# A graph-attention kernel in which the ORs of a mask check stand between a run's other steps, and chunk 0 masks a unit before it compares the next

## The reference: what is computed

```python
# layer 0: 4 heads of 32 features
Wh = (h @ W).reshape(N, H, D)
e = s_src[:, None, :] + s_dst[None, :, :]
e = where(e >= 0, e, 0.2 * e)
e = where(adj[:, :, None] > 0, e, -9e15)
attention = softmax(e, axis=1)
x = layernorm(x + elu(einsum('ijh,jhd->ihd', attention, Wh)))
# layer 1: one head of 128 features, between logmap0 and expmap0
e = leaky_relu(wh1 + wh2.T, 0.2)
attention = softmax(where(adj > 0, e, -9e15), axis=1)
x = layernorm(x + proj(expmap0(attention @ x_tan)))
```

## Time and profile before

| | |
|---|---|
| runs | 971.72, 972.5, 977.3 us; median 972.5 |
| profiled execution, its own time | 975.74 us |
| its span | 974.0 us |
| PE busy in the span | 856.1 us (88%) |
| DVE busy | 769.9 us (79%) |
| ACT busy | 674.0 us (69%) |
| mean granted TensorE clock | 0.956 |

### The profile page before, as it was taken

One profiled execution on the slowest core, in us unless ns is written; L12 is line 12 of the kernel. 1 busy time (PEld: TensorE's weight loads), 2 busy tenths in 40 slices (PEclk: granted clock), 3 DMA queues, 4 the chain that ended last, 5 costly groups with the idle time before them and its releaser, 6 DMA issues.

```text
span 974.0 us, 24352 instructions
## 1 busy us (share of the span) xinstructions
PE 856.1 (88%) x10868; PEld 698.2 (72%) x10868; DVE 769.9 (79%) x1312; ACT 674.0 (69%) x789; POOL 43.3 (4%) x80
## 2 busy tenths in 40 slices
PE   8468999989999899999998994899999999879890
PEld 6467999989999899999997952455555555445450
DVE  3857898899988999889976897868565858575865
ACT  3868988888999879999889864873845444426101
POOL 2200000000000000000000000000000010100000
PEclk9879999999999999999999997899999899989995
DMA  8988278704568036040301040202032424241320
GB/s 143 172 83 207 61 72 95 223 23 48 68 75 229 24 38 75 25 196 24 104 9 24 2 152 1 87 23 98 11 109 71 168 81 158 95 159 43 104 87 13
DMA packets 41906, 84.66 MB, mean 87 GB/s; under 512 B 6211, under 2 KB 31173, under 8 KB 41157
## 3 DMA queue, kind: packets, MB, share of 16 engines
q0 software_dynamic: 12416, 33.56, 23.7%
q1 hardware_dynamic: 29380, 49.50, 14.4%
HBM read 112.27 MB, written 21.12 MB: 137 GB/s over the span
## 4 chain that ended last, share of the span: by engine, by line
PE 51%; DVE 27%; ACT 14%; issue 4%; DMA 3%; SPq 0%; DVEq 0%; ACTq 0%
PE bank L610 32%; PE bank L982 9%; ACT masks L692 9%; PE bank L969 6%; DVE ring L558 4%; DVE ring L577 3%; DMA moving<-masks_kept 3%; ACT ring L545 2%; PE bank L461 2%; ACT masks L448 2%; DVE ring L735 1%; DVE ring L587 1%; DVE ring L716 1%; DVE ring L581 1%; ACT moving L498 1%
## 5 line engine op out<-in xcount | busy, mean ns | idle before, releaser
L610 PE MATMUL bank<-moving,ring 128*128 128x99 bf16 (+1 forms) x6400 | 460.5, 220 | 11.6 <-DVE ring L587 7.9
L610 PEld LDWEIGHTS bank<-moving,ring 128*128 128x128 fp8e4 x6400 | 390.3, 98 | 15.3 <-DVE ring L587 8.8
L545 ACT ACTIVATE ring<-s_rows,scores 128x1024 fp8e4<-128x1024 f32 x356 | 377.5, 1142 | 15.6 <-PE bank L610 14.2
L610 PE MATMUL bank<-moving,masks 128*128 128x99 bf16 x1792 | 241.5, 209 | 28.5 <-DVE ring L577 17.2
L610 PEld LDWEIGHTS bank<-moving,masks 128*128 128x128 fp8e4 x1792 | 175.9, 98 | 30.9 <-DVE ring L577 18.1
L982 PE MATMUL bank<-moving,masks 128*128 128x387 bf16 x1152 | 195.9, 328 | 0.0
L982 PEld LDWEIGHTS bank<-moving,masks 128*128 128x128 fp8e4 x1152 | 112.9, 98 | 79.4 <-issue 0.5
L692 ACT ACTIVATE masks<-s_rows,adj_tiles 128x512 fp8e4<-128x512 f32 x256 | 157.8, 709 | 0.1
L336 ACT ACTIVATE ring<-ring 128x4 f32<-128x4 f32 x24 | 4.9, 205 | 190.1 <-DVE ring L292 157.2
L577 DVE SCALAR_TENSOR_TENSOR ring<-ring,masks 128x1024 int32<-128x1024 int32 x89 | 108.4, 1219 | 4.7 <-ACT ring L545 4.7
L587 DVE TENSOR_TENSOR ring<-masks,ring 128x1024 int32<-128x1024 int32 x72 | 88.2, 1225 | 26.3 <-PE bank L610 24.6
(11 more groups left out here) (179 smaller groups left out, 604.5 us busy)
## 6 DMA issues: line engine op xcount, KB each, us to landing
masks_kept<-masks SPq DMA_DIRECT2D x4, 4096.0 KB, 18.3
masks<-masks_kept SPq DMA_DIRECT2D x8, 2048.0 KB, 12.0
moving<-masks_kept POOLq DMA_DIRECT2D x32, 512.0 KB, 5.0
adj_tiles<-in_adj_dram POOLq DMA_DIRECT2D x24, 512.0 KB, 8.3
s_rows<-score_rows SPq DMA_DIRECT2D x14, 512.0 KB, 5.8
adj_tiles<-in_adj_dram POOLq DMA_DIRECT2D x16, 256.0 KB, 15.3
feat<-in_x_dram SPq DMA_DIRECT2D x4, 512.0 KB, 5.7
values_kept<-masks SPq DMA_DIRECT2D x1, 2048.0 KB, 14.3
```

The costliest lines, as they stand in the source:

```text
L545: last = act.activation(j_tile(below, k), s_rows[:, h % 2, :], ACT.Sign, bias=scores[:, g * JU + k, h:h + 1], saturate=False)
L610: last = pe.matmul(bank[b][:, at + lo:at + hi], mask, moving[:, j, h, lo:hi], start=first, stop=(j == T - 1), skip_group_check=True)
```

## The change

Four things are moved; no arithmetic is added or dropped.

- **Check.** In the rounds e = 2 to 6, one OR stands between `evacuate_run` and `finish_run` and one behind `finish_run`; in the rounds e = 1 to 5, one OR stands behind each of the four `split_group`. That is 4 ORs in round 1, 6 in each of rounds 2 to 5, and 2 in round 6, where the remaining 2 stand ahead of `raise_flag`.
- **Mask, then compare.** In head 0 of chunk 0, DVE masks unit u and then compares unit u + 1 (if that is DVE's); before it compared first. Everywhere else the compare stays ahead.
- **Heads 1 to 3.** DVE's three steps for head 1 stand behind units 0, 1 and 2; for head 2 all three behind unit 3, for head 3 all three behind unit 5 (before: two steps behind units 0, 2, 4 and the third behind 1, 3, 5). On ACT the two roundings of heads 1, 2, 3 stand together behind units 2, 3 and 4.
- **Quarters.** ACT takes quarter 2 behind unit 3 (before: 2), after the roundings of head 2, and quarter 3 behind unit 4 as before, after the roundings of head 3. PE turns quarter 3 ahead of unit 5 (before: 4).

```diff
--- before.py
+++ after.py
@@ -563,7 +563,8 @@
             h, g = divmod(u, UH)
             if g == 0:
                 wait_s(dve, c, u)
-            if g + 1 < UH and not ON_ACT[c * U + u + 1]:
+            compare_next = g + 1 < UH and not ON_ACT[c * U + u + 1]
+            if compare_next and (c > 0 or h > 0):
                 dve_compare(dve, c, u + 1)
             below = below_slot(c, u).bitcast(I32)
             m = masks[:, c % 2, :].bitcast(I32)[:, g * (JU * C // 4):(g + 1) * (JU * C // 4)]
@@ -585,6 +586,8 @@
                 dve.wait_ge(below_ready, above_count(c, u + 1))
                 wait_above_slot(dve, c, u)
                 dve.tensor_tensor(above_slot(c, u).bitcast(I32), m, below, ALU.bitwise_xor).then_inc(unit_ready, 1)
+            if compare_next and c == 0 and h == 0:
+                dve_compare(dve, c, u + 1)
 
         def pe_unit(pe, c, u):
             h, g = divmod(u, UH)
@@ -946,8 +949,8 @@
 
                 for c in range(NC):
                     for u in range(U):
-                        if c == 0 and u in (0, 2, 4):
-                            turn_quarter(pe, u // 2 + 1)
+                        if c == 0 and u in (0, 2, 5):
+                            turn_quarter(pe, {0: 1, 2: 2, 5: 3}[u])
                         for q in groups_at(c, u):
                             turn_group(pe, c + 1, q)
                         pe_unit(pe, c, u)
@@ -1027,11 +1030,10 @@
                                 act.wait_ge(kept, c * 16)
                             take_group(act, c + 1, q)
                         if c == 0:
-                            if u in (1, 3, 5):
-                                round_part(act, u // 2 + 1, 0)
-                            if u in (2, 4, 6):
-                                round_part(act, u // 2, 1)
-                            if u == 2:
+                            if u in (2, 3, 4):
+                                round_part(act, u - 1, 0)
+                                round_part(act, u - 1, 1)
+                            if u == 3:
                                 act.wait_ge(scores_out, 16)
                                 take_quarter(act, 2)
                             if u == 4:
@@ -1136,10 +1138,15 @@
                         if u % UH == TAKE_AT and u > UH:
                             take_head(step, c, u // UH - 1)
                         if c == 0:
-                            if u in (0, 2, 4):
+                            if u == 0:
+                                weigh_values(dve, 1)
+                            if u == 1:
+                                take_high(dve, 1)
+                            if u == 2:
+                                take_middle(dve, 1)
+                            if u in (3, 5):
                                 weigh_values(dve, u // 2 + 1)
                                 take_high(dve, u // 2 + 1)
-                            if u in (1, 3, 5):
                                 take_middle(dve, u // 2 + 1)
                         else:
                             if u == TAKE_AT:
@@ -1198,16 +1205,25 @@
                     if e == 0:
                         for g in range(2, NG):
                             split_group(dve, 1, g)
+                    if 2 <= e < NR - 1:
+                        check_part(dve, done)
+                        done += 1
                     finish_run(step, e)
+                    if 2 <= e < NR - 1:
+                        check_part(dve, done)
+                        done += 1
                     if e + 2 < NR:
                         for g in range(NG):
                             split_group(dve, e + 2, g)
+                            if e > 0:
+                                check_part(dve, done)
+                                done += 1
                     if e == 0:
                         begin_checks(dve)
-                    while done < CHECKS * max(e - 1, 0) // (NR - 3) and done < CHECKS:
-                        check_part(dve, done)
-                        done += 1
                     if e == NR - 2:
+                        while done < CHECKS:
+                            check_part(dve, done)
+                            done += 1
                         raise_flag(step)
 
         fast.close()
```

## The result

| | before | changed |
|---|---|---|
| median of the runs | 973.09 us (971.72 to 977.3) | 947.13 us (942.36 to 949.81) |
| profiled execution, its own time | 975.74 us | 942.36 us |
| its span | 974.0 us | 940.6 us |
| PE busy in the span | 856.1 us (88%) | 845.2 us (90%) |
| DVE busy | 769.9 us (79%) | 767.9 us (82%) |

The ratio is 0.9724, with a 95% interval of 0.9679 to 0.9769: faster by 2.3 to 3.2%. The forecast was 944.0 us in a range of 940 to 955. Run once more beside the one before, it took 947.51 us against 973.19, ratio 0.9733 [0.9707, 0.9759].

The account below looks back on a forecast made before the run. PE was held by DVE, late through its order, not its load. Gains of 27.1 (second layer) and 1.7 (chunk 0), 28.8 in all, gave 946.9 from the profiled 975.74, 943.7 from the median 972.5; forecast 944.0, range 940.0 to 955.0.

Parts of the forecast that it names:

- The second layer: PE works through its last four runs there without a pause, 42.6 us each, ending at 923.5 instead of 950.65: 27.1 us.
- if the clock's part stays: Second layer's lower bound, 16.5 us: the 6.6 us of lower-clock pieces stay and each of four pauses keeps 1 us.
- The spare time of a round: Second layer: DVE readies PE's next run 38.5 us into a round, PE comes at 42.6, so 4.1 us to spare.
- bare ORs that wait 7: Rival: a round's two uncovered ORs, ahead of the finish and behind the last masks, wait 3.5 us each; 959, chance 0.05.
- a row of scores later than 18.2: Slower rival: scores' row lands over 18.2 us after a run's end, PE waits; 984 if at 28 us, chance 0.02.
- Chunk 0: First layer's start: PE begins unit 8 near 97.3 instead of 99.02, winning 1.7 us; bounds -1.5 to 3.0.
- Seven microseconds won at unit 1 have shrunk: Chunk 0: 7 us won at unit 1 become half of one by unit 6's signs, given back through ACT's steps.
- the whole 28.8: Sum of 27.1 us from the second layer and 1.7 us from chunk 0.
- collide with the refill: Rival: check loads delay SP's refill of masks and scores' row in a round's first half; 955, chance 0.06.
- DVE stays late: Rival: second-layer rounds stay too long for an unseen reason, the gain falls to half; 958, chance 0.04.
- nothing changes: Rival: PE's pauses come from waiting for masks, not banks; chance 0.02, within 1% as a whole 0.03.
- the likeliest case: Both gains, in the second layer and chunk 0, come about; 941 to 949 us, chance 0.81.

Follow-up runs that it names:

- extra6: The changed kernel with six more ORs of the sum with itself ahead of the finish in each of rounds 2 to 5; 966.14 us, ratio 0.9907.
- stacked_nowait: The kernel before, ORs where they were, but only the first three of 32 check parts loaded, so ORs never wait; 963.15 us, ratio 0.9885.
- chunk0_only: The kernel before with chunk 0's edits as in the changed kernel, ORs where they were; 973.55 us, ratio 0.9987.

## Why the prediction was right, point by point

**The second layer (27.1 us forecast).** From PE's restart to the last product it is 337.5 us before and 310.6 after: 26.9. The windows are 42.60 at clock 1.00, the wait for the reductions is gone, and so are the waits for parts, as foretold. The round went by the sum to within half a microsecond, counted from 747.0:

| step | forecast | measured |
|---|---|---|
| finish starts | 2.3 | 2.1 |
| signs start (760.92) | 14.1 | 13.9 |
| last OR behind masks ends | 37.5 | 37.3 |
| reductions of tile 0 end, about | 38.5 | 38.1 |

**The split of the 27.1 was wrong, its total right.** The forecast wrote 20.5 for pauses and 6.6 for pieces at the lower clock, as if these were two losses to be won back apart, and set a lower bound "if the clock's part stays". extra6 shows that in a round which DVE sets the low clock lies inside the round. So of the 27.1, 25.5 was DVE's lateness (run 7 began at 906.39 in place of 753.1 + 3 x 42.6 = 880.9), and 1.6 the low clock of run 7 alone (44.26 - 42.6), behind which no round of DVE's stands. The lower bound of 16.5 takes 6.6 off for a clock's part that in runs 4 to 6 cost nothing. stacked_nowait divides the gain by cause: 11 to 14 us waits for parts, 12 to 14 place.

**The spare time of a round was mis-sized.** 4.1 us is right for a round that begins on time and was used as if it held for all; 2.5 is what lasts, since late reductions stand in a row. The change left the round inside both, so the forecast did not suffer. The rivals priced with 4.1 (bare ORs that wait 7, a row of scores later than 18.2) would have cost up to 1.6 us a round more than was said.

**Chunk 0 (1.7 us forecast).** Unit 8 starts at 96.89 against 97.3 forecast and 99.02 before: 2.1. The chain went in the order written, each step 0.4 to 1.2 early, since it began 1.2 early (signs of unit 1 ended at 37.4, not 38.6): unit 3 masked 51.1 (52.2), quarter 2 taken 60.8 (61.95), signs of unit 4 ended 65.0 (66.1), compare of unit 5 ended 69.0 (69.95), first side of head 3 weighed 71.4 (72.3), quarter 3 taken 79.9 (80.7), unit 6 on PE 85.45 (86.1). That the sum hit is partly luck: counted from the signs of unit 1 the changed order wins 0.9 in this profile and 2.1 in the second, where 1.7 was forecast. Small misses: unit 1 started at 43.8, not 42.5, in this execution, in which quarter 1 had been turned 1.9 us later than in the one before; and PE's wait for quarter 2 was 1.2 us and not 2 to 3; and with the durations given, unit 6 would end at 92.6 and not 92.8. Wrong was the reason for counting at unit 8, that "from 99.02 on PE works without a pause": from 99 to 565 us in the kernel before PE waits for DVE's masks (7.9 us, 6 times) and reductions (6.3, 7 times), at most 2.2 at once, and 5.1 us more without a releaser, so what is won at unit 8 need not reach the end. "Seven microseconds won at unit 1 have shrunk" is what happened. What the forecast listed, and did not draw a conclusion from, is that ACT "now waits for DVE" behind compare and mask of unit 5: that wait was the change's own doing. Undoing the mask-first edit shortens it by 2.8 us (6.51 to 3.74), and the kernel is 4.6 us faster.

**Where the forecast was 3 us too low.** Against its own execution it gave 946.9, and the profiled executions of the changed kernel were 942.36 and 946.51. Against the median it gave 943.7, and the medians were 947.13 and 947.51. The step that failed is the one that took the whole 28.8 from the median: median to median the gain is 25.7 to 26.0. The second profile accounts for its 29.2 (975.74 - 946.51) with 26.2 in the second layer and 2.6 at unit 8, so the terms hold between profiled executions; the profiled execution of before was slower than its median (975.74 against 972.5), which I took to be an offset common to both kernels. It need not be, if the second layer of the kernel before is itself shorter in its faster executions. Its two profiled forms (before, 337.5; chunk0_only, 338.1) are of executions of 975.74 and 973.71 us, and no execution near 972.5 was profiled, so this stays open. The slow pieces near 222 and 345 us, which come and go between executions at 1.6 us each, are another candidate that was not in the sum at all.

In the first profile the gain is 33.4, of which 26.9 + 2.1 is accounted for. Of the other 4.4, 4.2 lie between unit 8 and the end of the first layer (460.5 us before, 456.3 changed), where the change moves nothing. The two units that begin near 345 us take 10.14 us in the kernel before, with the window 340 to 350 us at clock 0.83, and 8.53 in the changed one, at 1.00: 1.6. The waits of PE from 500 to 540 us that have no releaser are 3.2 us before and 1.0 after: 2.2. The second profile of the same changed kernel takes 4.1 us more than the first there (460.4), and 4.0 of them are found in the same kinds of place: the pieces near 222 and 345 us take 10.12 and 10.14 in place of 8.50 and 8.53, and the waits without a releaser 1.8 in place of 1.0. So this is the execution's, not the change's.

**The rivals.** Loads did not collide with the refill: the row of scores issued at 747.6 landed in 10.0 us, between the 8.7 and the 14.0 of the earlier trace rows; one load of the check lay beside it (issued at 749.48; the one before, issued at 741.97, had landed after 3.9 us), and the forecast had been 9 to 12. All the rows of scores of the second layer landed in 8.6 to 10.2 us, and it cost nothing, as the signs start 13.9 us into the round. The Trainium skill, DMA: Bandwidth & Descriptors, section Issuing engines are not separate DMA queues, says that such transfers interleave; the trace agrees, 8.7 became 10.0. The landing:

```profile
DMA to landing us min/median/max: 10.0/10.0/10.0
```

The two bare ORs never waited for their parts. That DVE stays late, that the refill is late past 18.2, and that nothing changes did not come about. The chances of the likeliest case and of the rivals that are still faster add up to 0.96, where 0.94 was written for faster.

## What to carry to other kernels

Work of an engine that is off the critical path still belongs where that engine waits for somebody else: the same 32 ORs, with the waits for their data, cost 25 us behind the last wait of a round, and left PE no pause once they stood among its waits. Before two reorderings are put together, each is to be tried alone, since both may use the same idle time: here either edit of chunk 0 wins 5 to 7 us, and the two together 1 to 2. Spare time that is read from a round on schedule (4.1 us) is more than what lasts in a late one (2.5 us), because work that used to overlap the neighbour's last tile then stands in a row.

## What the runs showed of the hardware

Pauses of PE of 3.2 to 3.4 us in every round were each followed by a stretch at the lower of its two clock levels (1.2 against 2.4 GHz), which made a run of 42.6 us take 44.44 at mean granted clock 0.96; with pauses of 0.8 to 1.1 us the granted clock stayed 1.00 and the run 42.8. The prediction did not expect that such a stretch costs nothing where another engine sets the round (47.6 to 47.7 us, whatever PE's clock), and only counts in the last run (44.46, 1.9 more).

Two executions of the same kernel took 456.3 and 460.4 us from unit 8 to the end of the first layer. Of the 4.1 us, 3.2 are two stretches near 222 and 345 us, each behind the same 1.7 us wait for DVE in both: the granted clock of 219 to 232 us was 1.00 in one and 0.87 in the other, and two units took PE 8.5 or 10.1 us. What decides on this is not shown. A single profiled execution of this kernel is good to some 4 us there, which is more than the 1 to 2 us that the change's edits of chunk 0 give together, and about as much as what sets the moved heads apart.
